# Where GpSimd splits the down weights and writes out the tokens: its order at the end of an attention, and later side work in a tile loop

## The reference, cut to what matters

```python
h = _layernorm(x) * (1 + ca) + sa
x = x + ga * attention(h)                # layer 0: 16 heads of 16, softmax over 2048 tokens
h = _layernorm(x) * (1 + cb) + sb
logits = h @ router_w.T; top 2 of 8      # per token
x = x + gb * (experts(h) + shared(h))    # silu(h @ gate) * (h @ up) @ down
...
x = x + ga * _L1_attn_ref(h)             # layer 1, mod rows = silu(c1) @ wmod1
bw = where(w >= 0, 1, -1) * mean|w|
x = x + gb * (h @ bw.T + bias)
```

## Time and profile before

| | us |
|---|---|
| median of 3 runs | 1043.1 (1040.66 to 1044.41) |
| profiled execution, its own time | 1044.02 |
| its span, first to last instruction | 1042.2 |
| TensorE busy | 984.2 |
| VectorE busy | 864.3 |
| ScalarE busy | 678.3 |
| GpSimd busy | 354.4 |

### The profile page before, as it was taken

One profiled execution on the slowest core, in us unless ns is written; L12 is line 12 of the kernel. 1 busy time (PEld: TensorE's weight loads), 2 busy tenths in 40 slices (PEclk: granted clock), 3 DMA queues, 4 the chain that ended last, 5 costly groups with the idle time before them and its releaser, 6 DMA issues. The chain is left out here.

```text
span 1042.2 us, 19481 instructions
## 1 busy us (share of the span) xinstructions
PE 984.2 (94%) x7152; PEld 499.7 (48%) x7152; DVE 864.3 (83%) x1146; ACT 678.3 (65%) x1316; POOL 354.4 (34%) x364
## 2 busy tenths in 40 slices
PE   7999999999999999999999999998888879997867
PEld 5453433333333333333333333333367768996656
DVE  5588899999999999999999999982786563755786
ACT  3424777888888888888888888884633224543312
POOL 3386783120120511101101101267437620134553
PEclk9999899999999999999999999996889789998888
DMA  6799000151110110110110110200001233444311
GB/s 224 205 168 199 4 16 7 22 167 30 42 38 7 41 37 7 42 38 7 41 39 6 40 40 6 68 7 3 4 4 67 76 117 117 131 121 130 91 47 61
DMA packets 90131, 65.57 MB, mean 63 GB/s; under 512 B 48406, under 2 KB 77942, under 8 KB 89462
## 3 DMA queue, kind: packets, MB, share of 16 engines
q1 hardware_dynamic: 85334, 54.36, 20.8%
q0 software_dynamic: 3072, 8.39, 2.4%
q10 hardware_dynamic: 1632, 1.58, 0.4%
HBM read 34.93 MB, written 26.74 MB: 59 GB/s over the span
## 5 line engine op out<-in xcount | busy, mean ns | idle before, releaser
L1203 ACT ACTIVATE prob<-ps 128x512 f32<-128x512 f32 x1024 | 547.0, 598 | 117.0 <-PE ps L687 101.9
L1423 DVE TENSOR_REDUCE mxp<-ps 128x2 f32<-128x1024 f32 x480 | 579.5, 1222 | 14.6 <-PE ps L659 9.6
L687 PE MATMUL ps<-qst,kst 50*128 50x512 f32 x1024 | 370.3, 454 | 0.0
L659 PE MATMUL ps<-kst,qst 48*128 48x512 f32 x960 | 334.1, 451 | 0.0
L687 PEld LDWEIGHTS ps<-qst,kst 50*128 50x128 f32 x1024 | 156.5, 188 | 229.2 <-ACT prob L1203 208.4
L728 PE MATMUL ps<-prob,vp 128*32 128x256 f32 x2832 | 226.2, 391 | 0.0
L659 PEld LDWEIGHTS ps<-kst,qst 48*128 48x128 f32 x960 | 132.9, 186 | 12.6 <-issue 6.5
L728 PEld LDWEIGHTS ps<-prob,vp 128*32 128x32 f32 x2832 | 55.7, 108 | 130.5 <-issue 70.1
L2047 POOL TENSOR_TENSOR rec<-o_x,neg 128x16 f32<-128x16 f32 x16 | 46.7, 2917 | 167.5 <-DVE o_x L1444 167.3
L721 PE MATMUL ps<-prob,vp 128*32 128x512 f32 x632 | 89.8, 642 | 0.0
L1990 POOL CAST nmp<-nmx 128x16 fp32r<-128x16 f32 x16 | 3.1, 197 | 254.2 <-DVE nmx L1427 230.2
(11 more groups left out here) (263 smaller groups left out, 1269.2 us busy)
## 6 DMA issues: line engine op xcount, KB each, us to landing
qst<-q_parts SPq DMA_DIRECT2D x96, 64.0 KB, 2.5
xg<-x_slots SPq DMA_DIRECT2D x46, 128.0 KB
y_slots<-ysb SPq DMA_DIRECT2D x46, 128.0 KB
x_slots<-zero SPq DMA_DIRECT2D x10, 512.0 KB, 3.0
kst<-k_parts SPq DMA_DIRECT2D x18, 256.0 KB, 11.3
k_parts<-parts SPq DMA_DIRECT2D x8, 512.0 KB, 4.2
q_parts<-parts SPq DMA_DIRECT2D x8, 512.0 KB, 5.7
att_t<-att_u SPq DMA_DIRECT2D x256, 8.0 KB, 1.8
```

The source lines that it names most:

```text
L659: last = nc.tensor.matmul(ps[:, 2 * p + b, :], qst[rows, g, a, P * j:P * (j + 1)], kst[rows, GP * g + a, CH * m:CH * (m + 1)], start=True, ...
L687: nc.tensor.matmul(ps[:, score_bank(done), :], kst[rows, GP * g + k // 2, P * t:P * (t + 1)], qst[rows, g, k // 2, :], start=True, stop=Tr ...
L1203: nc.scalar.activation(prob[:, t % 2, k, :], ps[:, score_bank(u * (G * MT) + G * t + k), :], ACT.Exp, scale=DH ** -0.5).then_inc(p_s, 1)
L1423: nc.vector.tensor_reduce(own, ps[:, 2 * p:2 * p + 2, :], AX.X, ALU.max).then_inc(mx_read, 1)
```

## The change

It has four parts.

1. GpSimd's list. In unit 13 `tokens_by_row(0)` comes first, then only the rounding `d_hi`. The subtraction `d_lo` becomes `down_rest`, behind `gate_attention(14)`, and it waits for chunk 1's `xh`. After unit 14 `deviation(1, 2)` comes ahead of `tokens_by_row(1)`.
2. The inverse of the softmax sums of units 14 and 15 is made by VectorE (`reciprocal`) instead of GpSimd (power).
3. TensorE does the logits and transposes beside the last unit one step later, and the second sort after the second `turn_in` instead of beside step 11 of the shared stage.
4. In the tile stage `wmod1` is loaded at tiles 4, 8, 12 instead of 0, 2, 4; the mod rows and what follows from them come six tiles later; the binarising comes one tile later.

```diff
-                if i in (0, 2, 4):
+                if i in (4, 8, 12):
                     sp.dma_start(wmod1_sb[:, :, cols], ...)
-                if i == 16:
+                if i == 22:
                     sp.wait_ge(row_ps, 3)
...
-                if 2 <= t < 6:
-                    logits(0, 2, 0, (t - 2,))
-                if t in (6, 7):
-                    turn1(1, t - 6)
+                if 3 <= t < 7:
+                    logits(0, 2, 0, (t - 3,))
+                if t in (7, 8):
+                    turn1(1, t - 7)
...
-                if n == 11:
-                    sort(1)
...
             turn_in(1)
+            sort(1)
...
-                if i in (8, 10, 12):
-                    row1((i - 8) // 2)
+                if i in (14, 16, 18):
+                    row1((i - 14) // 2)
...
+            def invert_sums(u):
+                dve.wait_ge(o_s, u + 1)
+                nc.vector.reciprocal(rec[:], o_x[:, :, DH]).then_inc(rec_s, 1)
...
             halves(0, 1, 1)
+            invert_sums(NU - 2)
...
             leave_output(NU - 1)
+            invert_sums(NU - 1)
             router(2, 5, 64)
...
-                if i == 22:
+                if i == 28:
                     bias_rows()
-                if i == 28:
+                if i == 29:
                     weight_mean()
...
-                pool.wait_ge(o_s, u + 1)
-                nc.gpsimd.tensor_tensor(rec[:], o_x[:, :, DH], neg1[:], ALU.pow).then_inc(rec_s, 1)
+                if u < NU - 2:
+                    pool.wait_ge(o_s, u + 1)
+                    nc.gpsimd.tensor_tensor(rec[:], o_x[:, :, DH], neg1[:], ALU.pow).then_inc(rec_s, 1)
...
+            def down_rest():
+                pool.wait_ge(xh_s, TPC * (ln(1, 1) + 1))
                 nc.gpsimd.tensor_tensor(d_lo[:], d_raw[:], d_hi[:].bitcast(F32), ALU.subtract).then_inc(down_s, 1)
...
                 if u == NU - 2:
                     input_rest(0)
-                    tokens_by_row(0)
                     deviation(1, 1)
...
+                if u == NU - 2:
+                    down_rest()
                 add_attention(u)
...
                 if u == NU - 3:
+                    tokens_by_row(0)
                     down_rounded()
...
             input_rest(1)
+            deviation(1, 2)
             tokens_by_row(1)
-            deviation(1, 2)
```

More of the change, by code:

```diff
@@ L535, in _ @@
                     load_tile(i + 6)
-                if i in (0, 2, 4):
-                    cols = slice(CH * (i // 2), CH * (i // 2 + 1))
+                if i in (4, 8, 12):
+                    cols = slice(CH * (i // 4 - 1), CH * (i // 4))
                     sp.dma_start(wmod1_sb[:, :, cols], wmod1_v[:, :, cols]).then_inc(mod1_in, 16)
-                if i == 16:
+                if i == 22:
                     sp.wait_ge(row_ps, 3)
@@ L817, in beside_last @@
                     turn1(0, 1)
-                if 2 <= t < 6:
-                    logits(0, 2, 0, (t - 2,))
-                if t in (6, 7):
-                    turn1(1, t - 6)
[L822 to L825, removed]
+                if 3 <= t < 7:
+                    logits(0, 2, 0, (t - 3,))
+                if t in (7, 8):
+                    turn1(1, t - 7)
+                if 11 <= t < 15:
+                    logits(1, 2, 32, (t - 11,))
+                if t in (14, 15):
+                    turn1(2, t - 14)
             unit(NU - 2, 2, 1, beside=beside_last_but_one, halved=range(2, MI - LEAD))
@@ L1044, in beside_tile @@
             def beside_tile(i):
-                if i in (8, 10, 12):
-                    row1((i - 8) // 2)
-                if i == 33:
+                if i in (14, 16, 18):
+                    row1((i - 14) // 2)
+                if i == 34:
                     l1_weights()
@@ L1817, in beside_tile @@
                     broadcast_c(1, cb1)
[L1818 to L1827, removed]
-                if i == 22:
+                if i in (15, 17, 19):
+                    row1((i - 15) // 2)
+                if i in (20, 22):
+                    gate_signs(rows1[:, (GA1, GB1)[(i - 20) // 2], :], mrow1[:, (2, 5)[(i - 20) // 2], :], rows1[:, TMP1, :])
+                if i in (21, 23):
+                    gate_sizes(rows1[:, (GA1, GB1)[(i - 21) // 2], :], rows1[:, TMP1, :])
+                if i in (24, 26):
+                    columns_product((i - 24) // 2)
+                if i in (25, 27):
+                    columns_sum((i - 25) // 2)
+                if i == 28:
                     bias_rows()
-                if i == 28:
+                if i == 29:
                     weight_mean()
-                if i == 29:
+                if i == 30:
                     weight_signs()
-                if i == 30:
+                if i == 31:
                     binarise()
-                if i == 31:
+                if i == 32:
                     detach()
-                if i == 32:
+                if i == 33:
                     attach()
-                if i == 34:
+                if i == 35:
                     leave_bw()
```

## The result

| | before | changed |
|---|---|---|
| median | 1043.76 us | 1035.63 us (4 runs, 1031.06 to 1037.58) |
| ratio | | 0.9891, 95% interval 0.9846 to 0.9935 |
| profiled execution, its span | 1042.2 us | 1033.2 us |

The kernel is 8 us faster by the medians. I had predicted 1028.8 us, a gain of 14.3: the direction was right, the gain too large by 6 us. The median of before here includes one run of 1052.7 us; without it it is 1043.1, the gain 7.5 and the miss 7. The size is known no better than to a few us: the ratio is not the quotient of the medians (that is 0.9922), and its interval allows a gain of 7 to 16 us.

What follows compares the result with a forecast made beforehand. TensorE, nearly always busy, was taken to lose time in waits on GpSimd's late work and the low clock behind them. Terms -12.8 - 3.0 + 1.5 = -14.3 us gave a median of 1028.8 us, range 1023 to 1036.

Steps and rivals of the forecast that it cites:

- the rival of the small gain: Clock falls for some three steps, tile-stage stall stays, binarising costs 4 us: -3 to -9 us, about 1037, chance 0.22.
- My own sign of being wrong: The prediction is wrong if the clock is low past step 7, or the gathers start later against the tiles.
- GpSimd's order in time: Last unit: `d_lo` runs 712.6 to 721.5; TensorE's 4.28 us wait and the low clock behind it go.
- The new wait: Last unit, step 7: `lg` ends with `d_lo`, at 721.9, so ScalarE's exponentials wait, a loss of 3.5 us.
- The term of the last unit: Shared stage begins at 747.5 instead of 757.55: -10.0 us, -12 at best, less if the clock falls at step 7.
- For unit 14 the gain is hidden: Unit 14's inverse on VectorE gains nothing, since its addition waits behind `d_lo` in any case.
- Unit 15's inverse: On VectorE 0.2 us instead of GpSimd's 2.92, all of it on the path to unit 15's addition.
- The addition of unit 15 and the shared stage: Unit 15's addition moves -12.8 us, to 772.1; the tile stage, through chunk 3's `hT_lo`, moves by the same.
- the term of -3.0 for the loads: First tiles: moving the `wmod1` loads shortens ScalarE's stalls by 3.0 us, bounds 0 and 6.9.
- a stall that stays: Rival at the first tiles: the loads have no part in ScalarE's stall, so the term is 0; no separate chance given.
- The term of +1.5 for the binarising: Late tiles: GpSimd's four additions fall over VectorE's binarising and block it: +1.5 us, bounds 0 and 5.

Runs made afterwards that it cites:

- after_again: The changed kernel once more, unaltered, with more runs: 1036.52 us, ratio 0.99 to the kernel before.
- exp_step9: The changed kernel with the router's exponential of chunk 0 ahead of step 9 instead of step 7 in ScalarE's list of the last unit: 1033.68 us, ratio 0.9872.
- order_only: The kernel before with GpSimd's order and TensorE's steps changed (parts 1 and 3) alone: 1039.65 us, ratio 0.9931.
- inverse14_back: The changed kernel with unit 14's inverse on GpSimd again, unit 15's still on VectorE: 1040.04 us, ratio 0.994.
- tokens2_late: The kernel tokens_early with `tokens_by_row(2)` moved behind the scaling of unit 15: 1028.15 us, ratio 0.9841.
- tokens2_wait: As tokens2_late, but `tokens_by_row(2)` also waits until chunk 2's ranks are done: 1024.28 us, ratio 0.9785.
- inverse_only: The kernel before with the inverse of units 14 and 15 on VectorE (part 2) alone: 1040.82 us, ratio 0.9952.
- tiles_only: The kernel before with the changed tile stage (part 4) alone: 1049.12 us, ratio 1.002.
- early_old_tiles: The kernel tokens_early with the tile stage as before the change (part 4 undone): 1027.86 us, ratio 0.9844.
- act_shift: The changed kernel with 16 more 128x1 instructions in ScalarE's list at step 9 of the shared stage: 1035.85 us, ratio 0.9926.
- tokens_early: The kernel exp_step9 with both halves of `tokens_by_row(1)` behind `d_lo`, ahead of unit 14's addition: 1027.67 us, ratio 0.986.

## Why the prediction was right in direction and too large

**The number.** The median of 1035.63 us lies inside my range of 1023 to 1036 by 0.4 us, that of `after_again`, 1036.52, outside it. Inside or outside is luck here. The gain of 7.5 to 8 us is the one that I had given the rival of the small gain (-3 to -9 us, about 1037, chance 0.22), and two of its three conditions came true: the clock fell behind the wait at step 7, though for two steps and not three, and the stall of the tile stage stayed; the binarising cost nothing. My own sign of being wrong, a low clock past step 7, came true as well.

**GpSimd's order in time: right.** `d_lo` was to start at 712.6, and started at 711.76, or 713.4 with the 1.6 us offset added back. TensorE's 4.28 us went, and the steps up to 6 ran at the full clock.

**The new wait: right in size, wrong in reach.** `lg` ended with `d_lo` and cost ScalarE 3.65 us (3.5 predicted). The term of the last unit, -10.0, came out as -6.7. With the offset added back, the ranks of chunk 0 began at 729.8 instead of 727.7, the transpose of chunk 2's `xh` came at 744.7 instead of 742.4, and the shared stage at 750.8 instead of 747.5. So of the missing 3.3 us, 2.1 lie between step 7 and the ranks, at the low level behind TensorE's 2.28 us except for 0.2 to 0.5 by which `lg` ended late; 0.2 in the stretch from the ranks to the transpose; and 1.0 behind the wait of 1.38 us, again at the low level. The step of the prediction that failed is therefore the clock behind step 7: I had written "it is less if the clock falls again at step 7" and had put nothing for it into the sum. exp_step9 takes the wait and the fall away together and gives 3.1 us back, so the two are not priced apart.

The 0.2 us for the stretch from the ranks to the transpose hides a slip and a stroke of luck. The parts that I gave for it, 15.6 - 4 + 2.35 and as much again, make 16.3 us and 744.0, not 742.4; my 742.4 is what they give when counted from 726.0, ahead of the 1.6 us of VectorE. With its own parts the term of the last unit would have been -8.4. The stretch measured 14.9, because the ranks lost more than 4 us with the tokens as a neighbour: from their first instruction to the statistics it was 10.8 us before (735.44 to 746.24) and 5.5 after (728.17 to 733.65), while the tokens cost 2.6 ahead of `xh` and 2.1 in it, about as predicted.

The Trainium skill, "SBUF — State Buffer", section "Who interferes with whom", has a VectorE instruction with two SBUF inputs blocked against GpSimd's reading. The runs agree: in the changed kernel, order_only and inverse14_back `lg` took 3.23, 5.18 and 5.21 us, in each case up to the end of `d_lo`.

**"For unit 14 the gain is hidden": wrong.** My own time line left the power out ahead of `d_lo`, and so the -10.0 us contained its gain, while the sentence denied it. inverse14_back measures it: 2.4 to 2.8 us at unit 15's addition. It is a third of the net gain. Unit 15's inverse took 0.25 us on VectorE (0.2 predicted). What it is worth is the rest between order_only and inverse14_back, -4.3 to -6.0 at that addition, 1.7 us of the 2.8 predicted; two single executions can't tell that apart from 2.8.

**The addition of unit 15 and the shared stage.** Predicted -12.8, measured -8.8 and -8.4: 3.3 us of the difference come from the last unit, and the transfers took 13.22 us instead of 12.55. That the tile stage hangs on this addition was right. In all kernels but tokens2_late and tokens2_wait, `hT_lo` of chunk 3 follows it within 0.5 us, net, whatever TensorE did in between: inverse_only began the shared stage 2.2 us late and had the addition and `hT_lo` 1.0 and 0.9 us early.

**The tile stage: the term of -3.0 for the loads failed.** Neither test shows a gain (tiles_only, early_old_tiles), and the stall of 4.6 us stayed where it was when the loads were moved away from it. The rows showed two loads beside a stall, and nothing more. The rival, a stall that stays, came true. I had built it on the Trainium skill, "Runtime: NRT & Kernel Launch", section "Instruction fetch mechanics", which says that fetching code is mostly hidden; no run shows what the fetching does here, and act_shift, where ScalarE's place in its code moved and the stall didn't, speaks against code as the cause.

**The term of +1.5 for the binarising: right mechanism, given back.** VectorE's timeline under GpSimd's four additions:

```profile
915.39 1.26 DVE L1725 TENSOR_SCALAR bw<-w_sb 128x512 f32<-128x512 f32 x1
...
917.69 3.75 DVE L1730 TENSOR_SCALAR bw<-bw,alpha 128x256 f32<-128x256 f32 x2
```

Before they took 0.41 and 0.61 us, so 4.0 us are lost on VectorE. The tiles lose 2.6 us between 28 and 32 (net -8.6 to -6.0), but the first gather is at a net -8.6 again. It waits for the stores up to tile 30, and that one still comes at -8.6: only the tiles behind it are late. At the end no loss can be told: from the first gather to the end three kernels with the old tile stage (inverse_only, order_only, early_old_tiles) lose 1.3 to 1.6 us against before, the changed kernel's two executions 1.2 and 0.7.

**The sum.** -10.0, -2.8, -3.0 and +1.5 were predicted; -6.7, -2.1, 0 and 0 (no effect that can be told) were measured, which is -8.8 at unit 15's addition. The last 1.4 us go before the end (-7.4), or 0.3 us in the other execution (-8.4, -8.1).

## What to carry to other kernels

A long GpSimd instruction over SBUF can price a small VectorE instruction with SBUF operands under it at what is left of its own length; here it did so to `lg`, `pr` and the comparisons, which have two, and to some with one, though not under GpSimd's power. Don't ask how long the small one is; ask who waits for it, and move that waiting one in its list, or the long one into a gap in which VectorE works from PSUM or waits for transfers. Put into the sum what follows a wait on TensorE, not the wait alone: here a wait of 2.28 us brought 6.8 us at the low level, which cost about 2 us. The length of the wait alone doesn't decide it: behind 1.71 us ahead of the shared stage the clock fell in the changed kernel, behind 1.72 us at the same place in tokens_early it did not. And compare two traces from a point that the change can't have moved; here unchanged code spread over 5 us, more than most terms of the sum.

## What the runs showed that I had not expected

- The granted clock fell from 1.00 to 0.50 at 731.6 us (early_old_tiles) and 744.7 us (inverse_only) with TensorE busy for 9.88 and 10.00 of the 10 us ahead, and didn't in tokens_early with the same instructions and 9.87. One such fall made the shared stage 6.2 us later.
- Not all SBUF operands are alike. Before the change, the statistics (four `bn_st` of 128x256, one SBUF input) took 1.40 us under `d_lo` at 706.28, as elsewhere (1.41), and a reduction to `rank` 0.42 us under the tokens at 742.40, as elsewhere. Nor did GpSimd's power stretch anything: under its 2.90 us in order_only all four `xh` took 1.38 us, while under the tokens they took 3.44, and under its 2.92 us at 767.88 before the change `lg` took 0.19 us and the first comparison 0.43, both with two SBUF inputs.
- Under the same GpSimd instructions VectorE's operations that read PSUM keep their length. Beside the additions of 9.66 us, `hdt`, `hl` and `tl` took 0.34, 0.42 and 0.41 us as elsewhere, while the binarising with SBUF operands alone took three to six times its time.
- ScalarE stands 3.8 to 5.3 us ahead of the `sgt` of tile 3 in all 14 traces, put down to TensorE, "remote" or "issue" in turn. The loads and ScalarE's place in its code are ruled out by tiles_only and act_shift; its cause is open.
